# A graph attention and mixture-of-experts stack on one core: one indicator per tile and the whole mask's product in the first chunk

## The chip, the core and the metric

The kernel runs on one core of a Trainium2 chip: TensorE (PE, matmuls into eight PSUM banks of 512 f32 columns), VectorE (DVE), ScalarE (ACT), GpSimd (POOL), and SyncE (SP), which issues loads. Each runs its instructions in the order in which they are written and waits on semaphores for the others. The metric is the device time of one execution in microseconds; lower is better.

## The reference

2048 nodes of 128 features pass four layers, each added to its input after a layer norm. Cut to the one that the change touches, the first:

```python
Wh = (h @ W.T + b).reshape(N, H, D)                    # N = 2048, H = 4 heads, D = 32
src = jnp.einsum('nhd,hd->nh', Wh, a[:, :D])
dst = jnp.einsum('nhd,hd->nh', Wh, a[:, D:])
e = jax.nn.leaky_relu(src[:, None, :] + dst[None, :, :], negative_slope=0.2)
att = jax.nn.softmax(jnp.where(adj[:, :, None] == 1, e, NEG_INF), axis=1)
h_prime = jnp.einsum('ijh,jhd->ihd', att, Wh)
```

Then follow a mixture of 8 experts with the two best of each node (hidden width 512), a second attention layer with logits averaged over the heads, and a two-layer stack with 16 routed experts (width 256).

## The kernel before

**No exponential per pair.** exp(leaky_relu(s + d)) is exp(s) exp(d) where s + d > 0, and exp(0.2 s) exp(0.2 d) elsewhere. So a head's attention needs two 0/1 matrices per tile, mask times "above zero" and mask times "not above", each multiplied with its own scaled values. The values of a tile, head and side are `u`: three bf16 parts (PARTS = 3) of 33 columns (32 features and the denominator), VW = 99 columns. For one tile, head and both sides the 198 columns lie side by side.

**Tiling.** The 2048 target rows are worked on in C = 4 chunks of 512 (CT = 4 tiles of 128). For a chunk and a head, all 16 source tiles are gone through in Q = 4 quads of QT = 4. `maskT` holds the transposed adjacency in bf16. It is made row by row (`mask_rows(r)`, 16 rows of 128 targets): POOL issues a load of the integer row as bf16 into one of four slots (`load_rows`, L415), PE transposes 16 blocks of 128 into banks 6 and 7 (L551, products at L558), ACT copies each bank (L920, L924). Rows 0 to 3 are needed by chunk 0, rows 4 to 7 by chunk 1, and so on. `ROWS` (L274) says which rows stand behind which head of chunk 0.

**Indicators.** `indicate(c, h)` on DVE (L1329) fills, for each quad, buffer 0 with mask times "above" and buffer 1 with the mask minus buffer 0 (L1349). For quad 0 the first comes from four comparisons with the threshold `thr` (L1345). For quads 1 to 3 ACT first writes the logits, scaled by 2**40 and cut at zero, into buffer 1 (`above`, L1029, four activations at L1040), and DVE takes the minimum with the mask (L1337). The logits come from the source row `sbc[:, h, :]`, which PE spreads over the partitions (`source_row`, L576) and ACT copies (L938).

**Products.** `attend(h)` on PE (L583) multiplies per source tile four target tiles with two sides: 128 products of 99 columns per head into banks 0 and 1 (L595). Each quad waits for `s_ind`; `s_indf` tells that its buffers are free again. ACT copies both banks (`sums`, L947, at L955), DVE adds the parts, applies the scales, divides and adds to `x` (`merge`, L1387 to L1404).

**Order.** Before chunk 0 DVE makes the values of heads 0 and 1 (`split`, L286), then the bounds of the second attention layer's logits (L1376 to L1383), then quad 0 of head 0. Per head of chunk 0 (L1434) it runs the indicators, for heads 0 and 1 one more `split`, and the merge of the head before. ACT (L1059) runs per head: quad 1 of the next head's logits, `sums`, source row for chunk 1, then mask rows mixed with quads 2 and 3 of the next head. PE (L676): products, source row, mask rows. Behind the last merge of chunk 0 comes `norm` (L1280), which scales `xn` (L1265); PE transposes it and chunk 1 begins (`scores`, `first_layer`, L635), in which the expert layers of one chunk are mixed with the attention of the next. POOL, after the last row load, adds up small bias tables (L444 to L457) and sets `s_wc`, for which ACT waits before chunk 1 (L1073).

## Time and profile before

| | |
|---|---|
| three runs, median (lowest to highest) | 672.66 us (670.26 to 673.15) |
| profiled execution | 673.83 us, its span 672.0 us |
| busy, share of the span | PE 84%, weight load 65%, DVE 78%, ACT 58%, POOL 25% |
| mean granted TensorE clock | 0.924 of full speed |
| chain that ended last, by engine | PE 61%, DVE 21%, ACT 11%, issue 4% |

A share over the whole span mixes stages with different limits, so the stage of the change, from about 28 to 120 us, has to be looked at by itself: busy times by window, then the chain of waits through it, then each engine's instructions in order of time.

### The profile page before, as it was taken

Reading aid. Unit: us, or ns where it says so; the run is one execution under the profiler, and the core shown is the slowest. Engines: PE = TensorE matmul, PEld = TensorE weight load, DVE = VectorE, ACT = ScalarE, POOL = GpSimd, SP = SyncE. Lnnn points to the kernel's source line nnn. Section 1 sums busy time; section 2 is a strip of 40 time slices with the busy share of each in tenths; the row PEclk is TensorE's granted clock in tenths of the full one; section 3 lists DMA queues with packets and bytes.
Section 4 is the critical chain, followed back from the end, with each engine's and each line's share of the span. In section 5 each row is a group of like instructions: output and inputs, shape, how many; then the busy total and the mean of one; then the engine's idle time right before and its main releaser. Section 6 shows DMA issues by size and latency. Waiting matters only on the chain.

```text
span 672.0 us, 13354 instructions
## 1 busy us (share of the span) xinstructions
PE 564.5 (84%) x5144; PEld 433.6 (65%) x5144; DVE 522.4 (78%) x900; ACT 390.5 (58%) x783; POOL 168.1 (25%) x186
## 2 busy tenths in 40 slices
PE   1835767899999999999998899989999755799985
PEld 1624756587787688776875765567879555457743
DVE  6699998876857874699939836697998999999530
ACT  1767789477787677876747645554341301465563
POOL 4200005010111010596151100022113000255741
PEclk9968898699999899998998989798999877799999
DMA  6553750002143343899498501001202825476660
GB/s 139 100 109 66 195 111 8 1 1 65 63 152 99 128 147 99 211 234 235 82 200 139 102 0 64 1 13 51 63 1 61 287 63 140 129 207 184 195 187 17
DMA packets 46373, 73.09 MB, mean 109 GB/s; under 512 B 4989, under 2 KB 24453, under 8 KB 46309
## 3 DMA queue, kind: packets, MB, share of 16 engines
...
## 4 chain that ended last, share of the span: by engine, by line
PE 61%; DVE 21%; ACT 11%; issue 4%; DMA 1%; POOL 0%; ACTq 0%; SPq 0%; DVEq 0%
PE bank L635 13%; PE bank L595 11%; PE bank L647 10%; DVE arena L1476 8%; PE bank L780 5%; PE bank L826 4%; ACT arena L1040 4%; PE bank L725 4%; PE bank L817 3%; PE bank L580 3%; DVE arena L1349 3%; DVE arena L1337 2%; PE bank L741 2%; ACT ysb L997 2%; DVE arena L1345 1%
## 5 line engine op out<-in xcount | busy, mean ns | idle before, releaser
L1040 ACT ACTIVATE arena<-heads,nd 128x512 bf16<-128x512 f32 x192 | 122.3, 719 | 31.3 <-PE bank L595 31.3
L465 POOL TENSOR_TENSOR x<-x,ysb 128x512 f32<-128x512 f32 x36 | 70.7, 1963 | 261.0 <-ACT ysb L997 259.4
L595 PE MATMUL bank<-reg_b,arena 128*128 128x99 bf16 x2048 | 101.2, 212 | 15.1 <-DVE arena L1349 15.1
L595 PEld LDWEIGHTS bank<-reg_b,arena 128*128 128x128 bf16 x2048 | 99.4, 100 | 18.0 <-issue 15.0
L635 PE MATMUL bank<-hTc,arena 128*128 128x512 f32 x192 | 95.7, 654 | 5.6 <-ACT reg_c L986 5.6
L1476 DVE SCALAR_TENSOR_TENSOR arena<-reg_b,nd,arena 128x1536 f32<-128x1536 f32 x48 | 90.8, 1955 | 0.0
L647 PEld LDWEIGHTS bank<-arena,reg_c 128*128 128x128 f32 x768 | 87.5, 192 | 4.8 <-issue 4.8
L1337 DVE TENSOR_TENSOR arena<-maskT,arena 128x2048 bf16<-128x2048 bf16 x48 | 61.3, 1277 | 36.9 <-ACT arena L1040 36.9
L1349 DVE TENSOR_TENSOR arena<-maskT,arena 128x2048 bf16<-128x2048 bf16 x64 | 87.0, 1359 | 2.2
L647 PE MATMUL bank<-arena,reg_c 128*128 128x128 f32 x768 | 87.8, 275 | 0.0
L986 ACT ACTIVATE reg_c<-bank,b 128x512 f32<-128x512 f32 x96 | 65.3, 687 | 26.7 <-PE bank L635 26.7
L635 PEld LDWEIGHTS bank<-hTc,arena 128*128 128x128 f32 x192 | 39.5, 210 | 55.8 <-issue 47.3
L997 ACT ACTIVATE ysb<-bank,comb 128x128 f32<-128x128 f32 x128 | 36.6, 368 | 63.3 <-PE bank L826 37.7
L725 PE MATMUL bank<-heads,arena 128*128 128x129 f32 x384 | 49.7, 296 | 16.2 <-DVE arena L1476 16.2
L725 PEld LDWEIGHTS bank<-heads,arena 128*128 128x128 f32 x384 | 49.2, 212 | 18.8 <-issue 18.8
L1345 DVE SCALAR_TENSOR_TENSOR arena<-heads,thr,maskT 128x512 bf16<-128x512 f32 x64 | 45.4, 770 | 12.6 <-PE bank L595 12.4
...
L1476 DVE SCALAR_TENSOR_TENSOR arena<-reg_b,nd,maskT 128x1536 f32<-128x1536 f32 x16 | 29.3, 1873 | 12.7 <-ACT reg_b L944 7.3
L558 PE MATMUL bank<-identb,reg_c 128*128 128x128 bf16 x256 | 21.7, 241 | 19.2 <-ACT maskT L924 16.5
L817 PE MATMUL bank<-hTc,arena 128*128 128x512 f32 x64 | 33.2, 668 | 0.9 <-ACT reg_c L1138 0.9
L558 PEld LDWEIGHTS bank<-identb,reg_c 128*128 128x128 bf16 x256 | 17.3, 107 | 25.6 <-issue 21.6
L580 PE MATMUL bank<-hT,wrep 128*128 128x512 f32 x64 | 32.1, 619 | 0.4 <-ACT hT L944 0.4
...
## 6 DMA issues: line engine op xcount, KB each, us to landing
...
routed_sums<-in_wrT POOLq DMA_DIRECT2D x32, 256.0 KB, 12.9
...
```

Source lines behind the costliest of these rows:

```text
L465: nc.gpsimd.tensor_tensor(xi, xi, ysb[:, e % 3, :].rearrange("p (t d) -> p t d", d=P), ALU.add).then_inc(s_acc, 1)
L580: mm(bank[b][:, :], wrep[:, h, :], hT[:, bass.ts(c, CW)], start=True, stop=True).then_inc(full[b], 1)
L595: last = mm(bank[i // 2][:, o:o + VW], ind[:, q, b, j, i * P:(i + 1) * P], u[:, (t * H + h) * 2 + b, :, :], start=(t == 0 and i % 2 == 0 a ...
L635: mm(bank[b][:, :], w1[:, s, e % 2, c * P:(c + 1) * P], hTc[:, :], start=True, stop=True).then_inc(full[b], 1)
L647: last = mm(bank[b][:, i * P:(i + 1) * P], hid[:, e % 2, c, i * P:(i + 1) * P], w2[:, s, e % 2, c, :], start=(c == 0), stop=(c == HC - 1))
L725: last = mm(bank[b][:, o:o + P + 1], wide[:, t % 4, i * P:(i + 1) * P], v1[:, t, :], start=(t == 0 and i % 3 == 0), stop=(t == T - 1), ski ...
L817: mm(bank[b][:, :], w1[:, e // 2 % 2, e % 2, c * P:(c + 1) * P], hTc[:, :], start=True, stop=True).then_inc(full[b], 1)
L986: af(hid[:, e % 2, c, :], bank[HB[c]][:, :], ACT.Relu, bias=b1[:, e, c:c + 1]).then_inc(ev["hid"], 1)
L1040: last = af(ind[:, q, 1, j, :], sbc[:, h, :], ACT.Relu, bias=nd[:, q * QT + j, h:h + 1], scale=BIG)
L1337: last = v.tensor_tensor(ind[:, q, 0, :, :], maskT[:, q * QT:(q + 1) * QT, cs], ind[:, q, 1, :, :], ALU.min)
L1349: v.tensor_tensor(ind[:, q, 1, :, :], maskT[:, q * QT:(q + 1) * QT, cs], ind[:, q, 0, :, :], ALU.subtract).then_inc(s_ind, 1)
L1476: last = v.scalar_tensor_tensor(p, row, nd[:, t, h:h + 1], p if h else maskT[:, t, columns], ALU.max, ALU.mult)
```

## The change

In chunk 0 only, DVE makes a single indicator per tile, mask times "above". Its two buffers now alternate between heads (`(h + 1) % 2`). PE multiplies it with both sides' values at once (`attend_first`, 64 products of 198 columns in two banks), and multiplies the mask itself with the "below" values (`attend_whole`, 64 products of 99 columns into bank 2). ACT copies that bank too (`whole_sums`), and `merge` subtracts the "above" part of it before it goes on. Quad 1 is made by comparison like quad 0, so ACT writes logits for quads 2 and 3 only, one head further ahead. The mask rows alternate between banks 6, 7 and 3, 5; row 4 stands before the first head's products, and the other rows partly before and partly behind the whole product of the next head. The bounds of the second layer's logits are computed in chunk 1. Counts of later waits are adapted.

```diff
--- before.py
+++ after.py
@@ -141,6 +141,7 @@
         u6 = u.rearrange("p (t h b) s v -> p t h b s v", t=T, h=H)
+        u2 = reg_b[:, :].bitcast(BF16).rearrange("p (g w) -> p g w", w=2 * VW)
         rows1 = reg_b[:, 0:H * WW].rearrange("p (h i) -> p h i", h=H)
...
@@ -198,6 +199,7 @@
         routing = sb("routing", [P, CW])
+        whole = routing[:, 0:CT * VW]
         combT = routing[0:E0, :].rearrange("e (t i) -> e t i", t=CT)
...
@@ -271,11 +273,12 @@
         NC = 8
-        ROWS = (range(4, 8), range(8, 10), range(10, 13), range(13, T))
+        ROWS = (range(5, 8), range(8, 11), range(11, 14), range(14, T))
+        MASK_BANKS = ((6, 7), (3, 5))
         HB = (2, 3, 6, 7)
         HT = (5, 6, 7)
-        BANK3 = C + (C - 1) * E0 + 1
-        BANK5 = (C - 1) * (E0 // 2 + 1) + len(range(0, E0 * HC, len(HT))) + C
+        BANK3 = T // 2 + C + (C - 1) * E0 + 1
+        BANK5 = T // 2 + (C - 1) * (E0 // 2 + 1) + len(range(0, E0 * HC, len(HT))) + C
         FFN_Y = C * (E0 + 1)
...
@@ -414,7 +417,7 @@
                 if r >= 4:
-                    pool.wait_ge(full[7], r - 3 + (2 if r < 12 else 3))
+                    pool.wait_ge(full[5 if r % 2 else 7], (r - 4) // 2 + 1 + (0 if r % 2 else 2 if r < 12 else 3))
                 pool.dma_start(adj[:, r % 4, :], a["adj"][r * P:(r + 1) * P, :]).then_inc(s_adj[r % 4], 16)
...
@@ -601,6 +604,36 @@
                         last.then_inc(s_indf, 1)
+            def attend_whole(h):
+                pe.wait_ge(s_u, h + 1)
+                use(2, "att")
+                for t in range(T):
+                    for i in range(CT):
+                        last = mm(bank[2][:, i * VW:(i + 1) * VW], maskT[:, t, i * P:(i + 1) * P],
+                                  u[:, (t * H + h) * 2 + 1, :, :], start=(t == 0 and i == 0), stop=(t == T - 1),
+                                  skip_group_check=True)
+                last.then_inc(full[2], 1)
+            def attend_first(h):
+                use(0, "att")
+                use(1, "att")
+                for q in range(Q):
+                    pe.wait_ge(s_ind, k.event("ind"))
+                    for j in range(QT):
+                        t = q * QT + j
+                        for i in range(CT):
+                            o = i % 2 * 2 * VW
+                            last = mm(bank[i // 2][:, o:o + 2 * VW], ind[:, q, (h + 1) % 2, j, i * P:(i + 1) * P],
+                                      u2[:, t * H + h, :], start=(t == 0 and i % 2 == 0), stop=(t == T - 1),
+                                      skip_group_check=True)
+                            if t == T - 1 and i % 2:
+                                last.then_inc(full[i // 2], 1)
+                    if q < Q - 1:
+                        last.then_inc(s_indf, 1)
             def scores(src=xn):
...
@@ -673,13 +706,18 @@
                 mask_rows(r)
+            pe.wait_ge(ev["mask"], 2 * CT)
+            attend_whole(0)
+            mask_rows(CT)
             for h in range(H):
-                pe.wait_ge(s_u, h + 1)
-                attend(h)
+                attend_first(h)
                 source_row(h, 1)
-                for r in ROWS[h]:
+                for r in ROWS[h][:2]:
+                    mask_rows(r)
+                if h < H - 1:
+                    attend_whole(h + 1)
+                for r in ROWS[h][2:]:
                     mask_rows(r)
...
@@ -919,7 +957,7 @@
                 for half in range(2):
-                    b = 6 + half
+                    b = MASK_BANKS[r % 2][half]
                     got(b)
...
@@ -943,6 +981,14 @@
                        bias=nmx[:, h:h + 1], scale=SLOPE).then_inc(ev["rows"], 1)
+            def whole_sums():
+                v = k.at("sums")
+                if v:
+                    act.wait_ge(s_attf, v)
+                got(2)
+                af(whole, bank[2][:, 0:CT * VW], ACT.Copy).then_inc(ev["att"], 1)
             def sums(*widths, to=att):
...
@@ -1030,30 +1076,34 @@
-                if isinstance(n, int) and n == 0:
-                    pass
-                elif q < Q - 1:
-                    act.wait_ge(s_indf, n * (Q - 1) + (q + 1 - (Q - 1)))
-                else:
-                    act.wait_ge(full[1], n)
+                b = (n + 1) % 2 if n < H else 1
+                user = n - 2 if n <= H else n - 1
+                if user >= 0 and q < Q - 1:
+                    act.wait_ge(s_indf, user * (Q - 1) + q + 1)
+                elif user >= 0:
+                    act.wait_ge(full[1], user + 1)
                 for j in range(QT):
-                    last = af(ind[:, q, 1, j, :], sbc[:, h, :], ACT.Relu, bias=nd[:, q * QT + j, h:h + 1],
+                    last = af(ind[:, q, b, j, :], sbc[:, h, :], ACT.Relu, bias=nd[:, q * QT + j, h:h + 1],
                               scale=BIG)
                 last.then_inc(s_above, 1)
             def head(c, h):
-                if c * H + h + 1 < C * H:
+                if c and c * H + h + 1 < C * H:
                     above(c * H + h + 1, (h + 1) % H, 1)
+                if c == 0:
+                    whole_sums()
                 sums(4 * VW, 4 * VW)
                 if c < C - 1:
                     source_row(h)
             for r in range(CT):
                 mask_rows(r)
-            for q in range(1, Q):
-                above(0, 0, q)
+            for h in range(2):
+                for q in (2, 3):
+                    above(h, h, q)
+            mask_rows(CT)
             act.wait_ge(s_xb, C)
...
@@ -1062,12 +1112,12 @@
                 rows = list(ROWS[h])
-                for q in (2, 3):
-                    for r in rows[q - 2:q - 1]:
+                quads = ((2, 3), (2, 3), (1, 2, 3), ())[h]
+                for j in range(3):
+                    for q in quads[j:j + 1]:
+                        above(h + 2, (h + 2) % H, q)
+                    for r in rows[j:j + 1]:
                         mask_rows(r)
-                    above(h + 1, (h + 1) % H, q)
-                for r in rows[2:]:
-                    mask_rows(r)
             act.wait_ge(s_w2, 16 * NW2)
...
@@ -1326,6 +1376,23 @@
             then(v.tensor_tensor(bsum[:, :], bac[:, 0:H], bac[:, H:2 * H], ALU.add))
+            def indicate_first(h):
+                for q in range(Q):
+                    to = ind[:, q, (h + 1) % 2, :, :]
+                    if q < 2:
+                        if h >= 2:
+                            dve.wait_ge(s_indf, (h - 2) * (Q - 1) + q + 1)
+                        for j in range(QT):
+                            t = q * QT + j
+                            last = v.scalar_tensor_tensor(to[:, j, :], sbc[:, h, :], thr[:, t, h:h + 1],
+                                                          maskT[:, t, 0:CW], ALU.is_gt, ALU.mult)
+                    else:
+                        dve.wait_ge(s_above, 2 * h + q - 1)
+                        last = v.tensor_tensor(to, maskT[:, q * QT:(q + 1) * QT, 0:CW], to, ALU.min)
+                    last.then_inc(s_ind, 1)
             def indicate(c, h, quads=range(Q)):
...
@@ -1333,19 +1400,22 @@
                     if q:
-                        dve.wait_ge(s_above, n * (Q - 1) + q)
+                        dve.wait_ge(s_above, 2 * H + (n - H) * (Q - 1) + q)
+                        if n == H and q < Q - 1:
+                            dve.wait_ge(s_indf, (n - 1) * (Q - 1) + q + 1)
+                        elif n == H:
+                            dve.wait_ge(full[1], n)
                         last = v.tensor_tensor(ind[:, q, 0, :, :], maskT[:, q * QT:(q + 1) * QT, cs],
                                                ind[:, q, 1, :, :], ALU.min)
                     else:
                         dve.wait_ge(ev["rows"], n + 1)
-                        if not (isinstance(n, int) and n == 0):
-                            dve.wait_ge(s_indf, (n - 1) * (Q - 1) + 1)
+                        dve.wait_ge(s_indf, (n - 1) * (Q - 1) + 1)
                         for t in range(QT):
                             last = v.scalar_tensor_tensor(ind[:, 0, 0, t, :], sbc[:, h, :], thr[:, t, h:h + 1],
                                                           maskT[:, t, cs], ALU.is_gt, ALU.mult)
                     last.then_inc(s_g, 1)
-                    dve.wait_ge(s_g, n * Q + (q + 1))
+                    dve.wait_ge(s_g, (n - H) * Q + (q + 1))
                     v.tensor_tensor(ind[:, q, 1, :, :], maskT[:, q * QT:(q + 1) * QT, cs], ind[:, q, 0, :, :],
...
@@ -1355,7 +1425,7 @@
-            then(v.tensor_scalar(thr[:, :, :], nd[:, 0:QT, :], -1.0, None, ALU.mult))
+            then(v.tensor_scalar(thr[:, :, :], nd[:, 0:2 * QT, :], -1.0, None, ALU.mult))
...
@@ -1373,22 +1443,29 @@
             split(v, 1, then)
-            dve.wait_ge(ev["bound"], 1)
-            then(v.tensor_tensor(wnorm[:, 0:H], wnorm[:, 0:H], wnorm[:, H:2 * H], ALU.max))
-            v.tensor_scalar(var[:, 0:H], wnorm[:, 0:H], float(P), None, ALU.mult)
-            then(v.tensor_scalar(var[:, H:H + 1], wnorm[:, 2 * H:2 * H + 1], float(P), None, ALU.mult))
-            inverse_root(H + 1)
-            then(v.tensor_tensor(var[:, 0:H + 1], var[:, 0:H + 1], rstd[:, 0:H + 1], ALU.mult))
-            v.tensor_scalar(nmx[:, 0:H], var[:, 0:H], -SLOPE, LIFT, ALU.mult, ALU.add)
-            v.tensor_scalar(nmx[:, H:H + 1], var[:, H:H + 1], -1.0, None, ALU.mult).then_inc(s_nmx, 1)
+            dve.wait_ge(ev["rows"], H)
             dve.wait_ge(ev["mask"], 2 * CT)
-            indicate(0, 0, range(1))
+            def score_bounds():
+                dve.wait_ge(ev["bound"], 1)
+                then(v.tensor_tensor(wnorm[:, 0:H], wnorm[:, 0:H], wnorm[:, H:2 * H], ALU.max))
+                v.tensor_scalar(var[:, 0:H], wnorm[:, 0:H], float(P), None, ALU.mult)
+                then(v.tensor_scalar(var[:, H:H + 1], wnorm[:, 2 * H:2 * H + 1], float(P), None, ALU.mult))
+                inverse_root(H + 1)
+                then(v.tensor_tensor(var[:, 0:H + 1], var[:, 0:H + 1], rstd[:, 0:H + 1], ALU.mult))
+                v.tensor_scalar(nmx[:, 0:H], var[:, 0:H], -SLOPE, LIFT, ALU.mult, ALU.add)
+                v.tensor_scalar(nmx[:, H:H + 1], var[:, H:H + 1], -1.0, None, ALU.mult).then_inc(s_nmx, 1)
             def merge(c, h):
                 n = c * H + h
-                dve.wait_ge(ev["att"], n * 2 + 2)
+                dve.wait_ge(ev["att"], 3 * (n + 1) if c == 0 else H + 2 * (n + 1))
                 a4 = att[:, :].rearrange("p (g s v) -> p g s v", s=PARTS, v=V1)
+                if c == 0:
+                    below = att[:, :].rearrange("p (t b w) -> p t b w", t=CT, b=2)[:, :, 1, :]
+                    then(v.tensor_tensor(below, whole.rearrange("p (t w) -> p t w", t=CT), below, ALU.subtract))
                 then(v.tensor_tensor(red[:, :, :], a4[:, :, 1, :], a4[:, :, 2, :], ALU.add))
...
@@ -1432,7 +1509,7 @@
             for h in range(H):
-                indicate(0, h, range(0 if h else 1, Q))
+                indicate_first(h)
                 if h in (0, 1):
                     split(v, h + 2, then)
...
@@ -1449,6 +1526,8 @@
                 gate(c - 1, c - 1 + C)
+                if c == 1:
+                    score_bounds()
                 for h in range(1, H):
```

Left out are lines that only adapt counts (`load_pair`, two waits on the attention sums) and the size of `thr`.

## Rows read from the trace of the kernel before

**Rows 1.** Busy us (count) per window: PE, PEld, DVE, ACT, POOL; clock, DMA share, GB/s.
```profile
40.20:105.07 64.87, 41.61 (x608) 37.00 (x609) 61.64 (x91) 48.05 (x72) 4.22 (x8) 0.78 0.51 108
...
134.90:513.00 378.10, 359.56 (x3145) 277.12 (x3142) 287.36 (x447) 239.27 (x479) 89.76 (x72) 0.96 0.40 96
```
**Rows 2.** Chain that ended last, from 89 us: start, us, what.
```profile
89.85 1.64 PE bank L595 x32
91.49 0.94 PE bank L580 x2
...
95.84 2.44 ACT arena L1040 x4
```
**Rows 3.** DVE in order of time: start, us, instruction, [idle before it and its releaser].
```profile
40.20 0.16 DVE L1377 TENSOR_TENSOR wnorm<-wnorm 128x4 f32<-128x4 f32 x1
...
43.06 2.73 DVE L1345 SCALAR_TENSOR_TENSOR arena<-heads,thr,maskT 128x512 bf16<-128x512 f32 x4
...
54.15 1.29 DVE L291 TENSOR_TENSOR maskT<-arena,bd 128x512 f32<-128x512 f32 x2
...
59.54 2.73 DVE L1345 SCALAR_TENSOR_TENSOR arena<-heads,thr,maskT 128x512 bf16<-128x512 f32 x4
...
108.61 0.45 DVE L1392 TENSOR_TENSOR red<-att 128x264 f32<-128x264 f32 x1 [0.30 <-ACT att L955]
...
118.30 1.11 DVE L1265 TENSOR_SCALAR xn<-x,means,rstd 128x128 f32<-128x128 f32 x4
```
**Rows 4.** The subtraction's group, 40 to 119 us: busy us, mean ns.
```profile
L1349 DVE TENSOR_TENSOR arena<-maskT,arena 128x2048 bf16<-128x2048 bf16 x16 | 19.6, 1225 | 0.5
```
**Rows 5.** DVE in chunk 1, head 1, in order of time.
```profile
144.68 1.22 DVE L1337 TENSOR_TENSOR arena<-maskT,arena 128x2048 bf16<-128x2048 bf16 x1 [1.53 <-ACT arena L1040]
...
148.85 1.22 DVE L1337 TENSOR_TENSOR arena<-maskT,arena 128x2048 bf16<-128x2048 bf16 x1 [1.68 <-ACT arena L1040]
```
**Rows 6.** L595: a window (PE, PEld, clock, DMA, GB/s), chain row, timeline row.
```profile
47.20:51.40 4.20, 4.20 (x51) 4.20 (x52) 0.50 0.02 4
...
134.87 5.78 PE bank L595 x128
...
47.20 6.42 PE L595 MATMUL bank<-reg_b,arena 128*128 128x99 bf16 x96 [11.09 <-DVE arena L1349]
```
**Rows 7.** ACT in order of time: eight mask copies, two copies of sums.
```profile
29.86 7.41 ACT L924 ACTIVATE maskT<-bank 128x1024 bf16<-128x1024 bf16 x8
...
107.62 0.89 ACT L955 ACTIVATE att<-bank 128x396 f32<-128x396 f32 x2 [0.20 <-PE bank L595]
```
**Rows 8.** DVE, last merge and norm of chunks 0 and 1, in order of time.
```profile
111.57 1.13 DVE L1404 TENSOR_TENSOR x<-x,odiv 128x128 f32<-128x128 f32 x1
...
199.87 0.43 DVE L1392 TENSOR_TENSOR red<-att 128x264 f32<-128x264 f32 x1 [0.54 <-ACT att L955]
...
202.14 0.29 DVE L1404 TENSOR_TENSOR x<-x,odiv 128x128 f32<-128x128 f32 x1
...
207.47 2.73 DVE L1345 SCALAR_TENSOR_TENSOR arena<-heads,thr,maskT 128x512 bf16<-128x512 f32 x4
```
**Rows 9.** POOL in order of time, and the view of line 444 (ns, first and last start).
```profile
58.97 0.53 POOL L418 DMA_DIRECT2D reg_c<-in_adj  x1 [21.90 <-PE bank L558]
...
96.81 0.53 POOL L418 DMA_DIRECT2D reg_c<-in_adj  x1 [1.74 <-PE bank L558]
106.58 1.26 POOL L444 TENSOR_TENSOR ysb<-ysb 128x512 f32<-128x512 f32 x1 [9.24 <-issue]
...
116.20 0.64 POOL L453 CAST bparts<-ysb 128x512 bf16<-128x512 f32 x1
...
L444 POOLq MODIFY_POOL_CONFIG  x2: 37/37/37, 97.4 to 97.4; - x2
```
**Rows 10.** Windows at half clock, columns as in rows 1.
```profile
82.30:85.60 3.30, 2.85 (x35) 2.88 (x36) 3.27 (x4) 3.30 (x6) 0.00 (x0) 0.50 1.07 286
...
113.00:129.90 16.90, 11.48 (x41) 8.11 (x42) 15.72 (x47) 8.62 (x13) 4.37 (x8) 0.50 0.01 1
```

10 lines of the change are left out of this document (5 added, 5 removed).

## The prediction

> **What bounds the kernel now.** I read the stage windows first, then the chain of waits, then each engine's timeline. The span falls into three parts [rows 1]. From 40.2 to 105.1 us, the four heads of chunk 0, DVE is busy 61.6 of 64.9 us, PE 41.6 and ACT 48.0: DVE bounds this part. From there to 119.4 us DVE does the last merges and the norm that opens chunk 1. From 134.9 to 513 us PE is busy 359.6 of 378.1 us. The chain says the same: up to 89.8 us it is nearly all DVE (indicators L1345, L1337, L1349, and splits), then PE, ACT and DVE take turns [rows 2]. So time taken from DVE in chunk 0 moves everything behind it, until ACT or PE is late in its place. Chunk 1 starts when its `xn` is scaled, at 119.4 us [rows 3]; I work out the new time of that point and leave the rest of the span as it is.
>
> **DVE: removed and added.** Per head the "below" subtraction goes: in all 16 x 1.225 us = 19.6 us [rows 4]. Quad 1 is no longer one L1337 (1.22 us [rows 5]) but four L1345. Four of those take 2.73 us [rows 3], so +1.5 us per head. `indicate_first` is thus 2 x 2.73 + 2 x 1.17 = 7.8 us, where a head took 11.1 us (43.06 to 54.15) [rows 3]: -3.3 us a head. The bounds work (40.20 to 43.06) leaves: -2.9 us. Each merge gains one subtraction of 396 f32 columns; one of 264 takes 0.45 us [rows 3], so about 0.6 us. DVE alone: -13.2 - 2.9 + 2.4 = -13.7 us before the tail.
>
> **Where the bounds work goes.** `score_bounds` now stands ahead of head 1 of chunk 1. There DVE later waits 1.53 and 1.68 us for ACT's scaled logits [rows 5]. 2.9 us later the q=1 pair ends near 146.1 instead of 143.2 us, the q=2 pair near 148.5, and q=3 waits until 148.85 as now. Cost zero; if that cover were gone, 2.9 us.
>
> **PE.** Per head 128 products of 99 columns become 64 of 198 and 64 of 99: 19,008 columns for 12,672. At the full granted clock (2.4 GHz) 128 take 5.78 us, 45 ns each; at 0.50 (1.2 GHz) 51 take 4.20 us, 82 ns [rows 6]. No row has 198 bf16 columns. The bounds are 45 ns (as for 99 columns) and 90 ns at full clock; I take 86, since 45 and 82 ns follow the columns divided by the clock. A head's products are 5.5 + 2.9 = 8.4 us for 5.8, +10.4 us in all. `attend_whole(0)` lies in PE's idle 11.1 us before 47.2 us [rows 6]: mask rows 0 to 3 are copied by 37.3 us [rows 7], so it runs from 37.4 to 42 us, partly at half clock, and row 4 goes to 43 us. The others stand between the mask rows.
>
> The Trainium skill ("TensorE: Matmul & The Clock Gate", section on the back-to-back issue gap) gives about 81 ns per matmul of 128 columns and 131 ns at 512 in a stream of weight loads and matmuls. By it (an estimate between its figures, some 77 and 91 ns) a head would cost 9.9 us before and 10.8 us after, +0.9 us. The trace has 45 ns for 99 columns and decides.
>
> **ACT.** It loses the quad-1 logits of heads 0 to 3: four activations take 2.44 us [rows 2], -9.8 us. It gains four `whole_sums` of 0.45 us (396 columns, like L955) [rows 7]. The order matters more. Scaled logits are now written two heads ahead, so behind head 2 stand three groups for chunk 1 (n = 4) and rows 11 to 13, all ahead of `sums` of head 3. A row is two copies, 1.85 us by the eight in 7.41 us [rows 7].
>
> **The new order, step by step.**
> 1. DVE head 0 from 40.2: 48.0. Split 2 (54.15 to 59.54 before, 5.4 us): 53.3. Head 1: 61.1. Split 3: 66.5. `below` and the two sums of merge 0 (0.6 + 0.9): 68.0.
> 2. Only then may ACT copy whole and sums of head 1 and the source row: 70.1. PE, whose row 8 needs the bank that this row holds, is late here. Rows 8 and 9, whole 2 and row 10 take 5.6 us at full clock, 7.8 with some at half: 77.9. `attend_first(2)`: 5.5, so 83.4. DVE's head 2 ends at 77.5, so PE is late, not DVE.
> 3. ACT: sums and source row of head 2: 84.8. Three groups of logits and three rows: 3 x 2.44 + 3 x 1.85 = 12.9, so 97.7. Whole and sums of head 3: 99.0. PE finished `attend_first(3)` near 95.5 and DVE stands idle from 91.8.
> 4. DVE merge 3 and norm. In chunk 1 that takes 199.87 to 207.47, 7.6 us; in chunk 0 it took 10.8 us (108.61 to 119.4), because single operations stretched from 0.29 to 1.13 us while POOL ran L444 to L457 [rows 3, 8, 9]. With 0.6 for `below`: 107.2 to 110.4 us. POOL's chain starts 9.2 us behind its last mask-row issue [rows 9], and that issue follows PE's row 11 (about 85 us), so it would run about 95 to 105 and hit most of the tail. I take 109.6 us.
>
> The sum: 119.4 - 109.6 = 9.8 us, of the 13.7 that DVE gives up. Run to run the granted clock changes at other points of the work; it stood at 0.50 from 82.3 to 85.6 us [rows 10], for one; one more or one fewer stretch like it moves PE by about 1.7 us. The scaled point of chunk 1 is followed by the same work (PE at 0.50 until 129.9 us [rows 10]).
>
> **Mask rows and POOL.** The rows rotate over four banks, and POOL's waits follow banks 7 and 5. Row 8's load is issued after PE's row 4 (43 us, not 59). The 22 us that POOL waited there [rows 9] shrink to some 7, and with the DMA engines busy 0.51 of the stage [rows 1] loads that start earlier are not late. SP's pair loads follow `s_u` = 4, at 66 instead of 76 us, still 40 us before their use. Nothing on these queues costs.
>
> **Base.** The profiled execution took 673.83 us (span 672.0), 1.2 us above the median 672.66 of the three runs. I subtract from the median: 672.7 - 9.7 = 663.0 us.
>
> **Rivals.**
> - *DVE sets the whole path.* If PE is never late at head 2 and ACT's twelve us lie elsewhere, DVE ends merge 2 at 91.8, sums 3 come at 92.7, and the scaled point is 101 to 104: -16 to -18 us, 656 us. For it: DVE is the fullest engine [rows 1]. Against: ACT's order in step 3 is fixed in the code.
> - *POOL's start-up holds the gain.* ACT waits for `s_wc` before chunk 1, and that is set at 116.8 us, 20 us after the last row issue [rows 9]; the 9.2 us gap in it has no named releaser. If POOL's chain stays where it is, ACT starts chunk 1 no earlier than 116.8 us, 2.6 ahead of today's scaled point: 670 us. Against it: the gap begins with a configuration command right behind the last issue, at 97.4 us [rows 9], and that issue moves forward by 11 us.
> - *A clean tail.* Is POOL's chain instead over, or held up, while the last merge and the norm run, step 4 gives 107.2 and 660 us, inside my range. The Trainium skill ("GPSIMD Engine Reference", key points) says that GpSimd shares its SBUF interfaces with VectorE, with contention when VectorE reads two SBUF inputs; by that rule both could be stretched wherever they overlap, and the trace's stretched operations agree.
> - *PE at half clock becomes the bound.* At 82 and 165 ns `attend_first` costs 10.6 us, a whole product 5.3, a mask row 1.7 (16 x 128 columns at the same rate), a source row 1.9 (twice 0.94 [rows 2]). From 43 us to the end of head 3: 4 x 10.6 + 3 x 5.3 + 9 x 1.7 + 3 x 1.9 = 79 us, so 122; with sums, merge and norm 132 to 134 us: +14, 686 us. At full clock the same work is 41 us. PE reaches the old 107.6 us when about 60% of it runs at half clock; the mean granted clock of the stretch is now 0.78 [rows 1], 44% at half. What speaks against it: each long run of L595 has brought the clock up, and there is more of it.
> - *The change does not give what it frees.* The round trip of step 2 (merge, ACT, PE) appears once in my sum. If each head pays its 3 us or so (heads 1, 2 and 3), the 9.7 us are eaten: 672 us.
>
> **How the numbers follow.** The forecast (663, own range 660 to 666.5, the clean tail in it) 0.69; DVE alone 0.13; POOL holds it 0.04; half clock 0.07; the gain eaten 0.07. The range goes down to 655.5, to hold the DVE case, and up to 668.5, which leaves out the half-clock case, the POOL case and the eaten gain, 0.18, and takes in a gain eaten by half. A change of 0.5%, 3.4 us, is about what this measurement tells from none. Faster: 0.69 + 0.13 = 0.82; same 0.04 + 0.07 = 0.11; slower 0.07.
>
> **What would show it.** In the changed kernel's DVE timeline a head's indicators take 7.8 us and an idle gap of 5 to 8 us stands before the last merge of chunk 0, released by ACT's sums; in its ACT timeline three groups of logits and rows 11 to 13 stand back to back ahead of it; PE's row 8 waits until about 70 us. The scale of chunk 1 falls near 109.6 us. A granted clock under 0.7 over the heads, 198-column products above 100 ns at full clock, or L457 later than 107 us would make the prediction wrong.

## The result, and the profile after

The changed kernel took 663.14 us (median of 4 runs, 662.39 to 664.81) beside 672.9 us of the kernel before on the same chip (4 runs, 670.26 to 674.3). The ratio is 0.9853, 95% interval 0.9825 to 0.9881: 9.8 us faster. The forecast was 663.0 us.

The profiled execution took 663.44 us with a span of 661.7; before it was 673.83 and 672.0. The difference of the spans is 10.3 us, and the stage tells where it is: from the start of chunk 0 to the first comparison of chunk 1 it was 79.13 us (40.20 to 119.33), and now it is 68.89 (40.09 to 108.98). All of the gain lies there.

The page of the kernel after: span and busy times.

```profile
span 661.7 us, 13348 instructions
...
PE 568.8 (86%) x5144; PEld 440.6 (67%) x5144; DVE 510.2 (77%) x900; ACT 380.9 (58%) x771; POOL 165.4 (25%) x186
```

The windows of the kernel after, with the columns of [rows 1]: chunk 0 up to the end of DVE's last indicator, the rest of the stage, and the stage as one window.

```profile
40.09:87.56 47.47, 39.97 (x550) 37.40 (x548) 46.64 (x71) 38.11 (x60) 4.22 (x8) 0.92 0.64 137
87.56:108.98 21.42, 11.09 (x132) 10.08 (x128) 12.78 (x43) 14.92 (x22) 10.26 (x15) 0.76 0.08 17
...
40.09:108.98 68.89, 51.05 (x677) 47.48 (x674) 59.42 (x113) 53.03 (x80) 14.48 (x23) 0.87 0.47 99
```

The same stage as one window in the kernel before:

```profile
40.20:119.33 79.13, 49.33 (x712) 43.16 (x712) 74.63 (x130) 61.95 (x92) 14.42 (x23) 0.78 0.42 89
```

Here is the whole account. DVE is busy 59.42 us instead of 74.63, 15.2 less; its idle time grew from 4.50 to 9.47 us, 5.0 more; what is left is 10.2. PE works longer (51.05 for 49.33) and its mean granted clock in the stage is higher, 0.87 for 0.78. Until 87.56 us DVE is nearly full (46.64 of 47.47). The idle time comes behind that point, in one piece, as DVE's timeline shows (start, us, instruction, idle before it and its releaser):

```profile
40.09 5.38 DVE L1389 SCALAR_TENSOR_TENSOR arena<-heads,thr,maskT 128x512 bf16<-128x512 f32 x8
45.39 2.35 DVE L1393 TENSOR_TENSOR arena<-maskT,arena 128x2048 bf16<-128x2048 bf16 x2
...
66.02 0.56 DVE L1468 TENSOR_TENSOR att<-routing,att 128x396 f32<-128x396 f32 x1
...
98.33 0.57 DVE L1468 TENSOR_TENSOR att<-routing,att 128x396 f32<-128x396 f32 x1 [7.61 <-ACT att L1001]
98.94 1.39 DVE L1469 TENSOR_TENSOR red<-att 128x264 f32<-128x264 f32 x1
...
107.95 1.11 DVE L1315 TENSOR_SCALAR xn<-x,means,rstd 128x128 f32<-128x128 f32 x4
108.98 2.73 DVE L1415 SCALAR_TENSOR_TENSOR arena<-heads,thr,maskT 128x512 bf16<-128x512 f32 x4
```

The first two lines are one head's indicators, 40.09 to 47.66: 7.57 us for the 11.1 of [rows 3]. L1468 is the new subtraction. Merge 3, the last one of chunk 0, starts at 98.33 after 7.61 us of idle time, where before it had waited 0.30 [rows 3]. The norm's scale starts at 107.95 instead of 118.30.

ACT's timeline of the same kernel says what DVE waits for:

```profile
67.55 0.50 ACT L991 ACTIVATE routing<-bank 128x396 f32<-128x396 f32 x1 [5.90 <-DVE red L1470]
...
84.17 2.55 ACT L1086 ACTIVATE arena<-heads,nd 128x512 bf16<-128x512 f32 x4
86.62 1.92 ACT L962 ACTIVATE maskT<-bank 128x1024 bf16<-128x1024 bf16 x2
...
92.68 2.56 ACT L1086 ACTIVATE arena<-heads,nd 128x512 bf16<-128x512 f32 x4
95.13 1.93 ACT L962 ACTIVATE maskT<-bank 128x1024 bf16<-128x1024 bf16 x2
96.94 0.51 ACT L991 ACTIVATE routing<-bank 128x396 f32<-128x396 f32 x1
97.32 0.91 ACT L1001 ACTIVATE att<-bank 128x396 f32<-128x396 f32 x2
```

From 84.17 on, three groups of chunk 1's logits (L1086) and three mask rows (L962) stand back to back, with no wait between them, and only then the two copies that merge 3 needs. PE had the products for them ready at 94.5 us, 2.8 us before ACT copies them, as its timeline shows:

```profile
69.38 2.74 PE L561 MATMUL bank<-identb,reg_c 128*128 128x128 bf16 x24 [5.28 <-ACT heads L976]
71.92 4.50 PE L613 MATMUL bank<-reg_b,maskT 128*128 128x99 bf16 x64
...
77.14 5.61 PE L629 MATMUL bank<-reg_b,arena 128*128 128x198 bf16 x64
...
89.05 5.60 PE L629 MATMUL bank<-reg_b,arena 128*128 128x198 bf16 x64
```

The last line ends at 94.5. The first is the one long wait of PE in the stage: it stands still for 5.28 us before row 8, for the bank that ACT's source row holds, which itself waited 5.90 us for DVE (L991 above). The chain of waits gives the 64 products of 198 columns that start at 77.31 a length of 5.45 us, 85 ns each at full clock:

```profile
77.31 5.45 PE bank L629 x64
```

POOL, in order of time:

```profile
84.83 0.53 POOL L421 DMA_DIRECT2D reg_c<-in_adj  x1 [6.70 <-PE bank L561]
94.19 1.26 POOL L447 TENSOR_TENSOR ysb<-ysb 128x512 f32<-128x512 f32 x1 [8.83 <-issue]
...
104.76 0.77 POOL L460 TENSOR_TENSOR chan<-chan,above_g 128x1 f32<-128x1 f32 x3
```

Its last row issue moved from 96.81 [rows 9] to 84.83, and its chain with it, to 94.19 until 105.53. So it still lies over DVE's tail: L1469 takes 1.39 us where it takes 0.43 in the other merges.

### The profile page after: what moved, and what is told of

It is laid out like the page before. It is cut to its first block, busy times and chain, and to the rows that moved or that the text cites. A ratio compares the mean times of both kernels' runs of the same rounds, so it can differ in the third digit from the quotient of the medians.

```text
span 661.7 us, 13348 instructions
## 1 busy us (share of the span) xinstructions
PE 568.8 (86%) x5144; PEld 440.6 (67%) x5144; DVE 510.2 (77%) x900; ACT 380.9 (58%) x771; POOL 165.4 (25%) x186
## 4 chain that ended last, share of the span: by engine, by line
PE 61%; DVE 16%; ACT 13%; issue 5%; DMA 2%; POOL 1%; SPq 1%; ACTq 0%
PE bank L668 12%; PE bank L680 10%; PE bank L598 9%; DVE arena L1555 8%; PE bank L818 5%; ACT arena L1086 4%; PE bank L864 4%; PE bank L763 4%; PE bank L583 3%; PE bank L855 3%; ACT ysb L1043 2%; PE bank L779 2%; DVE arena L1389 2%; PE bank L547 1%; DMA routed_sums<-in_wsT 1%
## 5 line engine op out<-in xcount | busy, mean ns | idle before, releaser
L1086 ACT ACTIVATE arena<-heads,nd 128x512 bf16<-128x512 f32 x176 | 111.9, 720 | 20.3 <-PE bank L598 20.3
L668 PE MATMUL bank<-hTc,arena 128*128 128x512 f32 x192 | 95.6, 654 | 5.6 <-ACT reg_c L1032 5.6
L680 PEld LDWEIGHTS bank<-arena,reg_c 128*128 128x128 f32 x768 | 87.5, 192 | 4.8 <-issue 4.8
L680 PE MATMUL bank<-arena,reg_c 128*128 128x128 f32 x768 | 87.8, 275 | 0.0
L668 PEld LDWEIGHTS bank<-hTc,arena 128*128 128x128 f32 x192 | 39.5, 210 | 55.8 <-issue 47.3
L598 PEld LDWEIGHTS bank<-reg_b,arena 128*128 128x128 bf16 x1536 | 70.8, 97 | 2.3 <-issue 1.7
L598 PE MATMUL bank<-reg_b,arena 128*128 128x99 bf16 x1536 | 71.8, 207 | 0.1
L1419 DVE TENSOR_TENSOR arena<-maskT,arena 128x2048 bf16<-128x2048 bf16 x48 | 69.3, 1443 | 1.6
L1408 DVE TENSOR_TENSOR arena<-maskT,arena 128x2048 bf16<-128x2048 bf16 x36 | 45.1, 1253 | 32.0 <-ACT arena L1086 32.0
L1415 DVE SCALAR_TENSOR_TENSOR arena<-heads,thr,maskT 128x512 bf16<-128x512 f32 x48 | 34.4, 778 | 12.5 <-PE bank L598 12.4
L864 PEld LDWEIGHTS bank<-arena,reg_c 128*128 128x128 f32 x256 | 29.5, 192 | 3.4 <-issue 1.9
L864 PE MATMUL bank<-arena,reg_c 128*128 128x128 f32 x256 | 30.0, 275 | 1.3 <-ACT ysb L1043 1.3
## 6 DMA issues: line engine op xcount, KB each, us to landing
routed_sums<-ident POOLq DMA_DIRECT2D x4, 1024.0 KB, 12.8
```

The costliest lines, as they stand in the source:

```text
L598: last = mm(bank[i // 2][:, o:o + VW], ind[:, q, b, j, i * P:(i + 1) * P], u[:, (t * H + h) * 2 + b, :, :], start=(t == 0 and i % 2 == 0 a ...
L668: mm(bank[b][:, :], w1[:, s, e % 2, c * P:(c + 1) * P], hTc[:, :], start=True, stop=True).then_inc(full[b], 1)
L680: last = mm(bank[b][:, i * P:(i + 1) * P], hid[:, e % 2, c, i * P:(i + 1) * P], w2[:, s, e % 2, c, :], start=(c == 0), stop=(c == HC - 1))
L864: last = mm(bank[4][:, i * P:(i + 1) * P], hid[:, e % 2, c, i * P:(i + 1) * P], w2[:, e // 2 % 2, e % 2, c, :], start=(c == 0), stop=(c == ...
L1086: last = af(ind[:, q, b, j, :], sbc[:, h, :], ACT.Relu, bias=nd[:, q * QT + j, h:h + 1], scale=BIG)
L1419: v.tensor_tensor(ind[:, q, 1, :, :], maskT[:, q * QT:(q + 1) * QT, cs], ind[:, q, 0, :, :], ALU.subtract).then_inc(s_ind, 1)
```

## The experiments

My theory of the result: DVE gives up some 14 us, and 5 to 8 of that come back as its wait before merge 3, because of two things in the order of the work. ACT writes chunk 1's logits ahead of head 3's sums, and DVE makes split 3 ahead of merge 0, which holds up PE's row 8. What else the change does (the bounds moved, four banks, more columns on PE) has a price that can be taken one at a time. The rivals were that DVE sets the path alone, that PE does, and that POOL does.

The runs of one kernel lie up to 9 us apart, and a part of that may arise in chunk 3, far from the change (last section). So I read every experiment by marks in its own trace as well: from the first DVE instruction of chunk 0 (the first indicator, or the bounds where they come first) to merge 3, and to the start of the scale.

| kernel | start | merge 3, idle before it | scale starts | start to scale | median us | ratio to before, 95% |
|---|---|---|---|---|---|---|
| before | 40.20 | 108.61, 0.30 | 118.30 | 78.10 | 672.9 | 1 |
| after | 40.09 | 98.33, 7.61 | 107.95 | 67.86 | 663.14 | 0.9853 (0.9825 to 0.9881) |
| e1 ACT's order | 39.90 | 95.26, 4.75 | 104.96 | 65.06 | 660.12 | 0.9827 (0.9793 to 0.9861) |
| e2 merge first | 40.86 | 95.98, 4.49 | 105.60 | 64.74 | 659.61 | 0.9831 (0.9787 to 0.9874) |
| e3 both | 40.19 | 92.21, 1.40 | 101.92 | 61.73 | 655.26 | 0.9755 (0.9722 to 0.9787) |
| e4 bounds back | 41.66 | 102.11, 6.96 | 111.66 | 70.00 | 664.5 | 0.9862 (0.9810 to 0.9914) |
| e5 two banks | 40.73 | 103.11, 11.75 | 112.14 | 71.41 | 667.57 | 0.9922 (0.9885 to 0.9959) |
| e6 before, bounds moved | 40.50 | 107.25, 1.31 | 116.46 | 75.96 | 670.58 | 0.9958 (0.9929 to 0.9987) |
| e7 both, POOL early | 41.12 | 101.09, 4.44 | 108.26 | 67.14 | 662.72 | 0.9842 (0.9785 to 0.9899) |
| e8 both, PE kept busy | 40.65 | 92.89, 1.61 | 102.61 | 61.96 | 656.65 | 0.9737 (0.9675 to 0.9800) |
| e9 both, no POOL work | 41.10 | 93.54, 1.80 | 100.72 | 59.62 | 656.82 | 0.9780 (0.9739 to 0.9820) |
| e10 quarter whole | 41.04 | 96.33, 4.67 | 105.84 | 64.80 | 665.49 (one run) | |
| e11 both, quarter whole | 40.31 | 90.98, none | 102.38 | 62.07 | 657.59 (one run) | |

The ratios of e1 to e9 are to runs of the kernel before on the same chip, whose medians are 672.75 us for e1 to e4, 673.46 for e5 to e8 and 670.31 for e9 to e11. e9, e10 and e11 leave out work whose result is needed, so they are prices and no kernels to use.

### ACT's order alone

```diff
-                quads = ((2, 3), (2, 3), (1, 2, 3), ())[h]
+                quads = ((2, 3), (2, 3), (), (1, 2, 3))[h]
...
-                        above(h + 2, (h + 2) % H, q)
+                        above(min(h + 2, H), (h + 2) % H if h < 2 else 0, q)
```

> Of the changed kernel, ACT's three groups of scaled logits for chunk 1 (n = 4) are written behind the sums of head 3 and no longer ahead of them. My theory (two waits keep part of DVE's gain back, and this is one: DVE stands idle 7.61 us ahead of the last merge of chunk 0 because ACT copies the sums of head 3 late, at 97.3 us, while PE had them at 94.5): the sums are copied right behind PE's products, at about 95.5 us, the last merge starts near 95.7 instead of 98.3, and the time falls by 2.7 us, to about 660.5. What the logits then cost is hidden: ACT stood idle 7.75 us before chunk 1. Rival (the logits are needed early: chunk 1's first indicators wait for them, or POOL's work stretches whatever stands at that time): the same time as the changed kernel within 1 us.

Merge 3 of this kernel, in DVE's timeline:

```profile
95.26 0.57 DVE L1468 TENSOR_TENSOR att<-routing,att 128x396 f32<-128x396 f32 x1 [4.75 <-ACT att L1001]
```

The idle time fell from 7.61 to 4.75 us, and the stage to the scale from 67.86 to 65.06: 2.8 us. Of ACT's 12.8 us of queue only these 2.9 had been ACT's own doing. The rest of the wait was behind PE, which finishes head 3's products as late as before.

### Merge 0 ahead of split 3

```diff
                 indicate_first(h)
-                if h in (0, 1):
-                    split(v, h + 2, then)
+                if h == 0:
+                    split(v, 2, then)
...
                 if h:
                     merge(0, h - 1)
+                if h == 1:
+                    split(v, 3, then)
```

> Of the changed kernel, DVE's merge of head 0 stands ahead of the values of head 3 (split 3) and not behind them. My theory (the second wait: ACT may copy the sums of head 1 only when merge 0 has read the ones before, at 67.5 us, and PE's row 8 stands 5.28 us for the bank behind it): the sums of head 1 are copied near 63 us, PE is no longer late at head 2, its products end near 78.3 instead of 82.6, and everything behind comes 4 us earlier: about 659 us. The idle time of DVE ahead of merge 3 shrinks to about 3.5 us. Rival 1 (ACT's copies of rows and logits fill its time anyway): under 1 us. Rival 2 (DVE's path alone counts, and the order of its work changes nothing in its sum): no change.

The same row here:

```profile
95.98 0.57 DVE L1468 TENSOR_TENSOR att<-routing,att 128x396 f32<-128x396 f32 x1 [4.49 <-ACT att L1001]
```

And PE's products of head 2:

```profile
72.87 2.22 PE L629 MATMUL bank<-reg_b,arena 128*128 128x198 bf16 x16 [2.41 <-DVE arena L1389]
75.43 4.97 PE L629 MATMUL bank<-reg_b,arena 128*128 128x198 bf16 x48 [0.34 <-DVE arena L1389]
```

This gives 3.1 us by the stage, where 4 were expected. PE's wait before row 8 fell from 5.28 to 0.24 us, but PE then waits 2.41 us for DVE's comparisons of head 2, and the granted clock is 0.55 from 73.2 to 76.6 us, so that the 64 products take 7.4 us where they took 5.6. They end 39.4 us behind the start instead of 42.5. ACT's queue begins behind them, so it and all that follows come 3.1 us earlier; DVE is still idle 4.49 us before merge 3, because the queue itself is as long as before.

### Both together

The edit is that of the last two.

> Both reorderings together. My theory: DVE then bounds the whole stage; merge 3 starts right behind merge 2, near 91 us instead of 98.3, so the time falls by 7 us to about 656, which is what the rival 'DVE sets the whole path' gave in the prediction. The granted clock stays at full speed between 68 and 75 us, as PE no longer waits there. Rival (POOL's bias work, which stretches single DVE operations in the tail, or the wait of ACT for it, becomes the bound): 658 to 660 us and chunk 1 waiting for POOL.

The new row 8 in PE's timeline, and merge 3 in DVE's:

```profile
64.44 1.51 PE L561 MATMUL bank<-identb,reg_c 128*128 128x128 bf16 x24 [0.24 <-ACT heads L976]
```

```profile
92.21 0.57 DVE L1468 TENSOR_TENSOR att<-routing,att 128x396 f32<-128x396 f32 x1 [1.40 <-ACT att L1001]
```

The stage is 61.73 us, 6.1 less than in the kernel after, a little more than the 2.8 and 3.1 us of the two edits by themselves. PE's row 8 now waits 0.24 us, and DVE is idle 1.40 us before merge 3, where I had expected no wait. This kernel beats both: 655.26 us, ratio 0.9755 to the kernel before, with an interval (0.9722 to 0.9787) below that of the change. It shows that the two orders held back those 6 us. One of them came with the change, which writes chunk 1's logits one head further ahead; the other, split 3 ahead of merge 0, stood in the kernel before as well. One expectation of mine fell: the clock did not stay up. From 72.6 to 75.7 us its mean was 0.53, behind a wait of 2.40 us for DVE, and the products of head 2 took 7.20 us instead of 5.61. These 1.6 us are about the 1.40 that DVE still waits; no run here keeps the clock up at that place, so this link is not shown.

### What the moved bounds are worth

In the changed kernel, the bounds back before the first indicator:

```diff
+            score_bounds()
             for h in range(H):
                 indicate_first(h)
...
-                if c == 1:
-                    score_bounds()
```

> Of the changed kernel, the bounds of the second layer's logits are computed again ahead of the first indicator, as before the change (2.9 us of small DVE operations). My theory (DVE's work up to merge 0 sits on the path in spite of its idle time later, since merge 0 releases ACT's sums, these PE's row 8, and so on): +2.9 us, about 666, and DVE's idle time ahead of merge 3 stays at 7.6 us. Rival (DVE has 7.61 us of idle time ahead of merge 3, so 2.9 us more work is absorbed): no change, idle time 4.7 us.

The runs of this kernel lie between 660.1 and 666.5 us, too far apart to set 664.5 against 663.14. The trace is sharper. The bounds take 41.66 to 44.52, 2.86 us, and merge 3 is reached after this:

```profile
102.11 0.57 DVE L1469 TENSOR_TENSOR att<-routing,att 128x396 f32<-128x396 f32 x1 [6.96 <-ACT att L1001]
```

From the start to merge 3 it is 60.45 us for 58.24: 2.2 of the 2.86 us reach merge 3, and the idle time before it shrank from 7.61 to 6.96. The missing 0.65 us is found on PE:

```profile
76.33 3.85 PE L613 MATMUL bank<-reg_b,maskT 128*128 128x99 bf16 x64
```

PE's row 8 comes 32.14 us behind the start for 29.29, so the full 2.85 us arrive there. The whole product of head 2 then took 3.85 us where it took 4.50 (3.02 at full clock), since less of it ran at half clock. That has nothing to do with the bounds, and it is a measure of how far these marks can be trusted. That the 2.86 us would be absorbed, since 7.61 us of idle time lie there, is refuted: that idle time is behind PE and ACT, and these in turn wait for DVE's merge 0, so DVE's delay passes through.

The same part alone, on the kernel before:

```diff
+            def score_bounds():
...
+                if c == 1:
+                    score_bounds()
```

> The kernel before with one part of the change alone: the bounds of the second layer's logits are computed in chunk 1. My theory (DVE's path bounds the heads of the kernel before, and in chunk 1 the 2.9 us lie in DVE's waits for ACT): -2.9 us, about 669.8; the scale of chunk 1 near 116.5 instead of 119.4. Rival (the cover in chunk 1 isn't there, or the tail is held by ACT and PE): no change, or chunk 1's products of head 1 start later by up to 2.9 us.

```profile
107.25 0.43 DVE L1395 TENSOR_TENSOR red<-att 128x264 f32<-128x264 f32 x1 [1.31 <-ACT att L955]
```

It gives 2.1 us by the stage (75.96 for 78.10), and 2.9 by the medians (670.58 of ten runs beside 673.46; ratio 0.9929 to 0.9987), where 2.9 were expected. The price in chunk 1 is nil in both kernels: from the scale of chunk 1 to that of chunk 2 it is 88.14 us before (118.30 to 206.44), and with the bounds inside it 87.37 here (116.46 to 203.83) and 88.02 after (107.95 to 195.97). So this move brought some 2 of the 10.3 us.

### What the four banks are worth

```diff
-        MASK_BANKS = ((6, 7), (3, 5))
+        MASK_BANKS = ((6, 7), (6, 7))
...
-                    pool.wait_ge(full[5 if r % 2 else 7], (r - 4) // 2 + 1 + (0 if r % 2 else 2 if r < 12 else 3))
+                    pool.wait_ge(full[7], r - 3 + (2 if r < 12 else 3))
```

> The changed kernel with the mask rows over banks 6 and 7 only, as before the change; where they stand in the programs stays as changed. My theory (with the whole product between the rows, PE passes row r + 1 only when ACT has copied row r, and the products behind it wait too): head 3's products wait for row 13, which waits for ACT's copy of row 12 (at 94.2 us in the changed kernel), so PE ends head 3 near 101 instead of 94.5, the last merge starts near 102 instead of 98.3: +4 us, about 667. Rival (the rows are far enough ahead, and the extra banks were not needed): within 1 us of the changed kernel.

PE's timeline of this kernel, two of its mask rows, and DVE's merge 3:

```profile
73.45 1.87 PE L561 MATMUL bank<-identb,reg_c 128*128 128x128 bf16 x16 [2.81 <-ACT maskT L962]
...
90.32 1.85 PE L561 MATMUL bank<-identb,reg_c 128*128 128x128 bf16 x16 [2.30 <-ACT maskT L962]
```

```profile
103.11 0.77 DVE L1468 TENSOR_TENSOR att<-routing,att 128x396 f32<-128x396 f32 x1 [11.75 <-ACT att L1001]
```

With two banks a second mask row waits until ACT has copied the first and written the logits in between. PE is held 2.3 to 2.8 us at a time, and head 3's products end at 102.0 instead of 94.5. The first 3 us of that fall into the time that ACT's queue takes anyway, and merge 3 comes 4.1 us later behind the start (62.38 for 58.24), as expected. So the four banks are not an ornament of the single indicator: about 4 of the 10 us hang on them.

### Is PE's whole product on the path?

A quarter of the whole product, 4 tiles instead of 16:

```diff
-                for t in range(T):
+                for t in range(T - QT, T):
```

> The changed kernel with only the last four source tiles in the whole mask's product: 16 products of 99 columns per head, not 64, so the below part is left incomplete. My theory (in the changed kernel PE is late at head 2, so the whole product of head 2, 4.3 us at 71.9 us, is on the path, while those of heads 0, 1 and 3 are hidden): head 2's products end 3.2 us earlier, the last merge starts near 95 instead of 98.3 us. Rival (PE's added work is hidden everywhere): the last merge at 98.3, counted from a first indicator at 40.1.

```profile
96.33 0.57 DVE L1468 TENSOR_TENSOR att<-routing,att 128x396 f32<-128x396 f32 x1 [4.67 <-ACT att L1001]
```

Merge 3 is reached 2.95 us sooner (55.29 for 58.24), where 3.2 were expected of one whole product that is three quarters gone. It took 4.50 us in PE's timeline above, for the most part at half clock, and takes 1.51 here: 2.99 us less. Each head has such a product, yet only the price of one is on the path: that of head 2, behind PE's 5.28 us of waiting. (One run; its clock was at half in other places too, so I lean on the size alone.)

The same with both orders mended:

> Both reorderings (e3_both), with the same 16 of 64 products left of each whole product. My theory (with the two waits gone, DVE bounds all four heads, and PE's added work is hidden): merge 3 starts 52.0 us behind the first indicator, as in e3_both, within 0.5 us. Rival (PE is close behind DVE everywhere, so that its added work costs 1 us or more): 51 us or less.

```profile
90.98 0.57 DVE L1468 TENSOR_TENSOR att<-routing,att 128x396 f32<-128x396 f32 x1
...
91.59 1.40 DVE L1469 TENSOR_TENSOR red<-att 128x264 f32<-128x264 f32 x1
```

Merge 3 now follows merge 2 with no wait at all, 1.35 us sooner (50.67 for 52.02). I had expected less than 0.5, and the rival 1 us or more, so the rival holds: DVE alone does not bound the mended kernel, PE is 1.4 us late at head 3. It brings nothing though. The tail from merge 3 to the next comparison took 12.43 us (90.98 to 103.41) for 10.74, since POOL's L447 (91.11 to 92.69 here) now fell beside the merge's first sum (1.40 us for 0.43) and single operations behind it were stretched as well, and the scale started 0.3 us later behind the start than in the kernel with both orders.

### What POOL's chain costs the tail

On the kernel with both orders, POOL's chain put behind row 7's load:

```diff
-            for r in range(4, T):
+            for r in range(4, 8):
                 load_rows(r)
...
+            for r in range(8, T):
+                load_rows(r)
```

> Both reorderings (e3_both), and POOL's bias work (its start-up of 8.8 us, then some 10 us) stands behind the load of row 7 instead of behind that of row 15, so it runs near 44 to 55 us and not in the tail. My theory (POOL's work stretches those DVE operations that it coincides with, above all two-input ones; in the tail they cost 2.1 us against the clean tail of chunk 1): merge 3 to the end of the scale takes 8.2 us instead of 10.7, but the DVE work between 44 and 55 us is on the path as well and pays about the same: 654 to 655.5 us in all. Rival 1 (the stretching is peculiar to the small operations of the tail): 653, with DVE's indicators and values as short as now. Rival 2 (rows 8 to 11 are loaded too late, near 55 us and after): PE waits for row 10 or 11, 657 us or more.

POOL's timeline of this kernel, then DVE's:

```profile
46.88 4.25 POOL L447 TENSOR_TENSOR ysb<-ysb 128x512 f32<-128x512 f32 x1 [11.05 <-issue]
...
65.66 1.95 POOL L460 TENSOR_TENSOR chan<-chan,above_g 128x1 f32<-128x1 f32 x3
67.92 2.35 POOL L421 DMA_DIRECT2D reg_c<-in_adj  x4 [0.30 <-POOL chan L460]
```

```profile
49.89 1.29 DVE L296 COPY maskT<-bd 128x32 f32<-128x32 f32 x1
...
55.19 8.75 DVE L1392 SCALAR_TENSOR_TENSOR arena<-heads,thr,maskT 128x512 bf16<-128x512 f32 x8
...
101.09 0.57 DVE L1471 TENSOR_TENSOR att<-routing,att 128x396 f32<-128x396 f32 x1 [4.44 <-ACT att L1004]
...
109.29 2.73 DVE L1418 SCALAR_TENSOR_TENSOR arena<-heads,thr,maskT 128x512 bf16<-128x512 f32 x4
```

The expected gain turned into a loss: 67.14 us from start to scale against 61.73 with both orders, and a ratio of 0.9842 against 0.9755. The tail is clean, 8.20 us (101.09 to 109.29). But the chain ran into DVE's work and both were stretched. L447 (46.88 to 51.13) stood beside the end of head 0's minima and the first part of split 2 and took 4.25 us instead of 1.26; a copy of that split took 1.29 us instead of 0.19 and ended at 51.18, just behind L447. DVE's eight comparisons of head 1 stood beside L453 to L456 and took 8.75 us instead of 5.38. The whole chain took 20.7 us instead of 11.3. Rows 8 to 11 were then loaded at 67.92 only, and PE waited 3.7 us for them. Merge 0 comes 4.9 us later behind the start than with both orders (25.42 for 20.54), all of it DVE's stretched work, and merge 3 comes 8.0 us later (59.97 for 52.02). So Rival 2 (657 us or more) comes nearest. My theory had the stretching, but took it for no more than the tail would give back. Moving the work moved the collision to a place where it costs more.

So I priced it with the chain left out:

```diff
+            nc.gpsimd.memset(bparts[:, :, :], 0.0).then_inc(s_wc, 1)
...
-            then(nc.gpsimd.tensor_tensor(brs, brs, bsr, ALU.add))
```

> Both reorderings (e3_both) without POOL's bias work behind the row loads: the summed bias table of the last layer is filled with zeros early and the channel numbers stay unadjusted, so the last layer's biases and its choice of them are left out. My theory (in the tail, single DVE operations stand while POOL's operations run): from the start of merge 3 to the end of the scale 8.2 us instead of 10.7, chunk 1 starts 2.5 us earlier than in e3_both, about 652.8 in all. Rival 1 (the stretching comes from something else, for instance ACT's copies or row loads): 10.7 us as before, 655.3. Rival 2 (chunk 1's start then waits for ACT's logits, which end 103.8 us in e3_both): about 1 us gained.

Merge 3 and the next comparison, DVE; then PE behind the scale:

```profile
93.54 0.57 DVE L1455 TENSOR_TENSOR att<-routing,att 128x396 f32<-128x396 f32 x1 [1.80 <-ACT att L988]
...
101.75 2.73 DVE L1402 SCALAR_TENSOR_TENSOR arena<-heads,thr,maskT 128x512 bf16<-128x512 f32 x4
```

```profile
105.64 0.59 PE L630 MATMUL bank<-wgT,hTc 128*128 128x8 f32 x2 [2.62 <-ACT hTc L942]
```

The tail is 8.21 us, for 10.74 with POOL's chain: the collision costs 2.5 us. The prediction had put 8.2 (7.6 and 0.6) for the clean tail. Most of that is given back at once, as Rival 2 had it: ACT is still at its three groups of logits, which the new order puts there, and copies `hTc` late, so that PE waits 2.62 us instead of 0.77. From merge 3 to PE's first gate product it is 12.10 us for 12.77. The ratio, 0.9780 beside 0.9755, shows no gain over the kernel with both orders.

### Keeping PE's clock up

On the kernel with both orders, 160 products that nobody reads, behind the last mask row:

```diff
+            for n in range(160):
+                last = mm(bank[2][:, 0:VW], maskT[:, n % T, 0:P], u[:, n % T * H * 2, :, :], start=True, stop=True)
```

> Both reorderings (e3_both), and 160 products of 99 columns whose results nobody reads stand on PE behind mask row 15, while it would wait for the scale of chunk 1 (from 94.4 to 103.1 us). They add work and change no result. My theory (the granted clock falls to 0.50 in that idle time and rises again only at about 113 us; the gate scores take 4.2 us at half clock where chunk 2's take 2.6 at full clock, the transposes 1.1 for 0.6): the clock stays at full speed through the start of chunk 1, and the time falls by 2 to 2.6 us, to about 653. Rival (the start of chunk 1 is paced by ACT's copies and waits, not by PE's clock): no change.

The clock in the tail, a window of this kernel and one of the kernel with both orders, and then PE's timeline of this one:

```profile
98.90:107.20 8.30, 5.83 (x90) 5.35 (x87) 7.89 (x21) 6.16 (x10) 3.98 (x7) 1.00 0.01 2
```

```profile
99.30:113.00 13.70, 9.10 (x25) 6.47 (x26) 12.80 (x32) 5.97 (x11) 2.89 (x7) 0.50 0.00 1
```

```profile
106.80 0.38 PE L644 MATMUL bank<-bg,ones 1*128 1x8 f32 x2
107.11 0.55 PE L643 MATMUL bank<-wgT,hTc 128*128 128x8 f32 x2
...
108.12 10.05 PE L668 MATMUL bank<-hTc,arena 128*128 128x512 f32 x16
```

The full clock was kept through the transposes and the first gate products. It fell at about 107.2 us, among the gate products, with PE at work; before that PE had stood still for 1.70 us ahead of the transposes and for 0.77 us ahead of the gate products. A pair of them takes 0.38 us at full clock and 0.59 at half. From the end of the scale to L668 it is 1.7 us less, but L668 then takes 10.05 us for 9.05, so 0.7 us is left where 2 to 2.6 were expected. The ratios (0.9737 and 0.9755) do not tell the two apart. So the clock did cost something, but the theory failed in that it did not stay up.

Two parts of the change have not been priced by a run of their own: quad 1 made by comparison, and the single indicator by itself. What is left for the change without the moved bounds, some 8 of the 10.3 us, is a difference.

## Why the prediction was right, point by point

- **DVE's order until the first merge.** Step 1 had head 0 done at 48.0, split 2 at 53.3, head 1 at 61.1, split 3 at 66.5 and the sums of merge 0 at 68.0. The trace has 47.66, 53.06, 60.63, 66.02 and 67.5. The head was mis-sized by 0.2 us (7.57 for 7.8), hence the small lead. DVE's busy time fell by 15.2 us rather than 13.7: four times 0.2 for the heads, 0.7 in a tail that is stretched a little less (10.04 us without `below`, for 10.72).
- **PE's round trip.** Step 2 had ACT's row copies done at 70.1, PE back at the products of head 2 at 77.9 and through at 83.4. The trace: row 8 at 69.38, 77.14, 82.6. The guess that some of it would run at half clock held: the clock stood at 0.50 from 68.6 to 75.0, and the 64 products of 99 columns took 4.29 us in the chain. It could have been less: behind the same wait of 5.28 us, e1 has 4.38 and e4 3.85 us where PE's timeline of this kernel has 4.50.
- **ACT's queue.** Step 3 had 12.9 us of logits and rows, and the sums of head 3 at 99.0; the trace has 84.17 to 96.9, 12.8 us, and 98.2. DVE's idle time, 5 to 8 forecast, is 7.61. This was the step that decided the size of the result, and the runs with the two orders confirm it from both sides: take the queue away and 2.8 us go, take PE's round trip away and 3.1 go, take both and 6.1 go.
- **The tail.** Step 4 lay between 8.2 and 11.4 us with 10.6 taken; it is 10.65 (98.33 to 108.98). That POOL's chain follows its last issue, and so would move along with PE's row 11, held (94.19 to 105.53, where 95 to 105 was said). That it is POOL which stretches the tail was an argument then; the run without POOL's work (8.21 us) shows it. The Trainium skill ("SBUF — State Buffer", section on the two separate sides) has a reason: one pair of ports is shared by the two engines, a VectorE instruction in a 2-port mode or with two SBUF inputs needs it, and whichever starts first holds it for its whole instruction while the other is fully blocked. The traces agree in that both sides lose time: with POOL's chain moved forward L447 takes 4.25 us for 1.26, and DVE's comparisons beside L453 to L456 take 8.75 us for 5.38. Which instruction held the ports at a given moment no trace here shows.
- **Costs put at nothing.** The bounds in chunk 1 cost nothing (88.02 for 88.14 us). Row 8's load was issued at 42.96, and SP's pair loads at 66.1, as said; neither is waited for.
- **PE's new product.** I had put 86 ns on 198 columns, from rows at 99; it is 85. The Trainium skill gives some 81 ns for 128 columns and 131 for 512, in the back-to-back section of "TensorE: Matmul & The Clock Gate"; an estimate on a straight line between these figures is 90 ns (the prediction has 91). The trace decides: 85 ns, close to 198 columns at 2.4 GHz (82.5 ns).
- **The rivals.** *DVE sets the whole path* gave 656 us and a scaled point of 101 to 104. It is refuted for this kernel by the 7.61 us. With both orders its numbers are nearly reached (the next comparison stands at 102.95 and the median is 655.3), though DVE still waits 1.40 us there. *POOL's start-up holds the gain* would have had `s_wc` set at 116.8; it was set behind L456, at 104.5. *PE at half clock* needed 60% of the work there, and the mean clock until 87.56 us was 0.92. *The gain eaten* needed the round trip at each head; over the heads PE waits more than 3 us once.

The agreement to 0.1 us is luck. The four runs of the kernel after lie 2.4 us apart by themselves, the forecast rests on a half-clock stretch that could have been a us longer or shorter, and the prediction takes off 9.7 us where its own sum is 9.8. The scaled point is the better measure: 109.6 was forecast and 108.98 measured, 9.8 us gained and 10.3.
